# An early-fusion network with two mixture-of-experts layers: plain float32 products on halves of the array's rows instead of high and low parts, and one expert per unit of work

## The reference, cut to what matters

```python
h = concat([patches @ W + b, table[ids] + positions])            # 16 x 548 x 64
h = h + attn0(layernorm(h))     # q, k, v; relu(q k^T * scale) v; a small feed-forward with a relu; layer norms
h = h + moe0(layernorm(h))      # 8 experts, top 1, capacity 1370 tokens per expert: 64 -> 256 -> 64, relu
h = h + attn1(layernorm(h))     # linear attention with grouped norms of k and v, projection, gelu
# moe1: every one of the 8 experts is computed for every token; the two best are weighed
xe = xn[None] * ln_g[:, None] + ln_b[:, None]
hid = gelu(einsum('end,edh->enh', xe, W1) + b1)                  # 64 -> 256
y = einsum('enh,ehd->end', hid, W2) + b2                         # 256 -> 64
h = h + (weights * take(y, top2)).sum()
```

## Time and profile before

| | |
|---|---|
| median of 3 runs | 995.72 us (994.87 to 998.15) |
| span of the profiled execution | 996.3 us |
| busy PE (matmul) | 834.4 us, 84% |
| busy DVE | 691.3 us, 69% |
| busy ACT | 560.5 us, 56% |
| busy POOL | 421.6 us, 42% |
| mean granted TensorE clock | 0.894 of 2.4 GHz |

### The profile page before, as it was taken

The page is one execution under the profiler, slowest core; times in us unless marked ns, Lnnn a source line. Parts: engine busy times, 40 slices in busy tenths (PEclk is TensorE's granted clock), DMA queues, the critical chain, the costliest instruction groups (busy, mean ns, idle before and its releaser), DMA issues.

```text
span 996.3 us, 17997 instructions
## 1 busy us (share of the span) xinstructions
PE 834.4 (84%) x5574; PEld 594.9 (60%) x5574; DVE 691.3 (69%) x2473; ACT 560.5 (56%) x1259; POOL 421.6 (42%) x441
## 2 busy tenths in 40 slices
PE   5799869999987549934589999999999999999995
PEld 3666646666664436614466676666766667666663
DVE  3758789898866525547767778787777777877542
ACT  1366635555543224412266767777777776777773
POOL 4554477674542620046635553455644453110110
PEclk9599879999986569965579999999999999999998
DMA  9700000000000023310000000000000000000000
GB/s 287 218 12 11 10 14 30 23 24 10 5 4 2 6 89 125 109 40 16 6 2 9 2 7 8 7 8 2 7 9 7 9 2 7 8 7 7 1 12 6
DMA packets 36328, 29.06 MB, mean 29 GB/s; under 512 B 18546, under 2 KB 31770, under 8 KB 35850
## 3 DMA queue, kind: packets, MB, share of 16 engines
q1 hardware_dynamic: 27226, 20.59, 6.8%
q0 software_dynamic: 7200, 5.16, 2.1%
q10 hardware_dynamic: 1808, 2.17, 0.6%
HBM read 16.23 MB, written 15.38 MB: 32 GB/s over the span
## 4 chain that ended last, share of the span: by engine, by line
PE 54%; DVE 8%; ACT 7%; issue 4%; DMA 0%; POOL 0%; ACTq 0%; POOLq 0%; DVEq 0%
PE psum L422 12%; PE psum L862 11%; PE psum L863 7%; PE psum L867 4%; PE psum L868 4%; PE psum L435 3%; PE psum L852 3%; PE psum L1039 2%; ACT L511 2%; ACT L464 1%; ACT scratch L511 1%; PE psum L1021 1%; PE psum L360 1%; DVE stats L1213 1%; PE psum L936 1%
## 5 line engine op out<-in xcount | busy, mean ns | idle before, releaser
L511 ACT ACTIVATE scratch<-psum,fb 128x292 f32<-128x292 f32 (+1 forms) x512 | 227.2, 490 | 51.3 <-PE psum L863 50.1
L862 PE MATMUL psum<-xs,fw_hi 128*128 128x292 f32 (+1 forms) x512 | 180.4, 362 | 27.7 <-ACT scratch L511 27.7
L862 PEld LDWEIGHTS psum<-xs,fw_hi 128*128 128x128 f32 x512 | 98.3, 192 | 88.2 <-ACT scratch L511 56.0
L422 PE MATMUL psum<-scratch,w_fw 128*64 128x292 f32 (+1 forms) x1024 | 148.6, 412 | 0.0
L863 PE MATMUL psum<-xs,fw_lo 128*128 128x292 f32 (+1 forms) x512 | 144.9, 293 | 0.0
L302 POOL DMA_INDIRECT uu<-expert_out,slot_i x80 | 84.1, 1051 | 68.7 <-DVE stats L1213 42.5
L852 PE MATMUL psum<-w_ident,hl 128*128 128x128 f32 (+1 forms) x400 | 72.9, 300 | 36.6 <-DVE hl L1222 26.3
L863 PEld LDWEIGHTS psum<-xs,fw_lo 128*128 128x128 f32 x512 | 99.6, 194 | 0.0
L815 POOL DMA_INDIRECT slots_buf<-hl,slot_i x80 | 79.7, 997 | 43.5 <-issue 26.3
L519 ACT ACTIVATE yt<-psum,w_fb 128x256 f32<-128x256 f32 (+1 forms) x128 | 62.6, 489 | 61.8 <-PE psum L422 61.8
L422 PEld LDWEIGHTS psum<-scratch,w_fw 128*64 128x64 f32 x1024 | 62.9, 138 | 42.6 <-issue 12.8
(11 more groups left out here) (289 smaller groups left out, 1996.6 us busy)
## 6 DMA issues: line engine op xcount, KB each, us to landing
slots_buf<-zeros SPq DMA_DIRECT2D x8, 704.0 KB, 8.0
scratch<-slots_buf SPq DMA_DIRECT2D x8, 704.0 KB, 4.4
expert_out<-scratch SPq DMA_DIRECT2D x8, 352.0 KB, 2.5
out<-H SPq DMA_DIRECT2D x16, 128.0 KB
X<-in_patches ACTq DMA_DIRECT2D x1, 1728.0 KB, 7.8
slots_buf<-hl,slot_i POOLq DMA_INDIRECT x80
uu<-expert_out,slot_i POOLq DMA_INDIRECT x80, 2.3
scratch<-in_fw SPq DMA_DIRECT2D x1, 1024.0 KB
```

What stands on the lines that cost most here:

```text
L422: last = pe.matmul(bank(6)[h * D:(h + 1) * D, 0:z - a], w["fw2"][:, (2 * p + h) * J + j, :], hid[(4 * n + 2 * j + h) % 8][:, 0:z - a], sta ...
L511: act.activation(hid[m % 8][:, 0:z - a], bank(up_bank(m))[:, 0:z - a], ACT.Gelu, bias=fb1[:, e * J + j:e * J + j + 1]).then_inc(sem("gelu" ...
L862: pe.matmul(dst, parts[0][:, cols], rhs, start=True, stop=False)
```

## The change

- No high and low parts any more. `turn` transposes pairs of slots: the stack `[128, 292]` has the channels of the even slots' tokens (0, 2, 4: 292 columns) on partitions 0 to 63 and those of the odd slots' (1, 3: 256 columns) on 64 to 127. A batch takes 3 transposes instead of 5. Weights are held twice, on both halves.
- Products over 64 channels are plain float32 matmuls of 64 rows, one per half (`by_sides`, `tokens_by`, `scores`, `q`), which write to different banks (`q`: to different halves of a bank).
- Removed: the casts and subtractions (`high1` to `high3`, `low1` to `low3`, `q_low`, `k_low`, `high_low`, the second half of `fold`), `split_weights`, the splitting of `ew1` and `fw1` in steps 9 and 10, the stage cut1 (16 + 8 steps). `slots_buf` has rows of 64 values instead of 128.
- Banks: TURN (0), FFN (1), WIDE (2, 3), SCORE (4, 5), MIX (6), QUERY (7, also the count), values in (0, 1). The gate uses WIDE. ACT's relu of a `scores(s)` is one operation over both banks.
- Second part: a unit is one batch and one expert, two hidden tiles of 292 + 256 tokens; gelu is one operation over two banks (2 x 292 columns). TensorE's order in a position is up, up, small stage "a", `down` of n-1, `back` of n-2, small stage "b". The orders of the small stages are changed on each engine; DVE does some ahead of `weigh` (`DVE_FIRST`), and mixed and route_b move to positions 6 and 7. `back` ends with a transpose of 64 rows.
- Middle part: `b_turn` has 2 transposes instead of 4; `b_down` and `b_back` have one bank instead of two.

```diff
-        def turn(pe, src, dst_bank, cols=(2 * D)):
-            for s in range(SLOTS):
-                rows = P if s < TXT else N_IMG
-                last = pe.transpose(bank(dst_bank, 2)[0:cols, s * P:s * P + rows], src[0:rows, s, :], ident[0:rows, 0:rows])
+        def turn(pe, src, k):
+            for i in range(3):
+                rows, cols = (P, 2 * D) if i < 2 else (N_IMG, D)
+                last = pe.transpose(bank(k)[0:cols, i * P:i * P + rows], src[0:rows, 2 * i:2 * i + cols // D, :].rearrange("p s c -> p (s c)"), ident[0:rows, 0:rows])
             return last
 
         def turn_back(pe, src, k):
             pe.transpose(bank(k)[:, 0:P], src[:, 0:P], ident[:])
             pe.transpose(bank(k)[:, P:2 * P], src[:, P:2 * P], ident[:])
-            return pe.transpose(bank(k)[0:N_IMG, 2 * P:2 * P + D], src[D:P, LEFT:RIGHT], ident[D:P, D:P])
-
-        def two(pe, dst, parts, rhs, cols=slice(None)):
-
-            pe.matmul(dst, parts[0][:, cols], rhs, start=True, stop=False)
-            return pe.matmul(dst, parts[1][:, cols], rhs, start=False, stop=True)
-
-        def tokens_by(pe, dst, stack, parts, cols):
+            return pe.transpose(bank(k)[0:N_IMG, 2 * P:2 * P + D], src[0:D, LEFT:RIGHT], ident[0:D, 0:D])
+
+        def by_sides(pe, k, weight, stack):
+            for h, z in enumerate(SIDES):
+                half = slice(h * D, (h + 1) * D)
+                last = pe.matmul(bank(k + h)[:, 0:z], weight[half, :], stack[half, 0:z], start=True, stop=True)
+            return last
+
+        def tokens_by(pe, k, stack, weight):
+            n = weight.shape[1]
             for s in range(SLOTS):
-                pe.matmul(dst[:, s, :], stack[:, s * P:(s + 1) * P], parts[0][:, cols], start=True, stop=False)
-                last = pe.matmul(dst[:, s, :], stack[:, s * P:(s + 1) * P], parts[1][:, cols], start=False, stop=True)
+                half, at0, rows = slot(s)
+                i = s // 2 * n
+                last = pe.matmul(bank(k + s % 2)[0:rows, i:i + n], stack[half, at0:at0 + rows], weight[half, :], start=True, stop=True)
             return last
...
+                for h, z in enumerate(SIDES):
+                    half = slice(h * D, (h + 1) * D)
+                    last = pe.matmul(bank(SCORE[h])[0:rows, 0:z], kst[b % 2][half, s % 2, at0:at0 + rows], qst[b % 2][half, 0:z], start=True, stop=True)
+                last.then_inc(sem("scores"), 1)
...
+            def up(n, j):
+                b, e = unit(n)
+                if n % POS == 0 and j == 0:
                     pe.wait_ge(sem("xs5"), b + 1)
...
+                banks.take(pe, (2 + 2 * j, 3 + 2 * j), sem("gelu"), J * n + j + 1)
+                k = (e * J + j) * P
+                by_sides(pe, 2 + 2 * j, w["fw1"][:, k:k + P], xs2[b % 2]).then_inc(sem("up"), 1)
...
                     if now:
-                        up(n, 0, 1)
...
+                        up(n, 0)
+                        up(n, 1)
+                    narrow("a")
+                    if before:
+                        down(n - 1, 0)
+                        down(n - 1, 1)
                     if 0 <= n - 2 < NB * POS:
                         back(n - 2)
-                    if now:
-                        up(n, 3)
-                    if before:
-                        down(n - 1, 0, 1)
+                    narrow("b")
...
-        PE_ORDER = (("norm5", 1, "t5"), ("fold", 2, "gram"), ("norm5", 2, "route"), ("kv", 3, "t4"), ("fold", 3, "gains_k"),
-                    ("fold", 4, "gains_v"), ("fold", 5, "by_q"), ("kv", 5, "kv"), ("fold", 6, "by_proj"), ("fold", 7, "proj"))
...
+        PE_ORDER = (("fold", 1, "b", "gram"), ("norm5", 2, "a", "t5"), ("fold", 2, "b", "gains_k"), ("kv", 3, "a", "t4"), ("fold", 3, "b", "gains_v"),
+                    ("norm5", 4, "a", "route"), ("fold", 4, "b", "by_q"), ("kv", 5, "a", "kv"), ("fold", 5, "b", "by_proj"), ("fold", 6, "b", "proj"))
...
+            def gelu(n, j):
+                b, e = unit(n)
+                act.wait_ge(sem("up"), J * n + j + 1)
+                if n >= 2:
+                    act.wait_ge(sem("down"), n - 1)
+                act.activation(hid[(J * n + j) % 4][:], both(2 + 2 * j), ACT.Gelu, bias=fb1[:, e * J + j:e * J + j + 1]).then_inc(sem("gelu"), 1)
...
+        DVE_FIRST = (("fold", 2, "gram_s"), ("fold", 3, "p1_s"), ("fold", 4, "own_heads"), ("fold", 5, "add_input"), ("fold", 6, "fold"), ("fold", 7, "pre_bias"))
+        DVE_ORDER = (("fold", 1, "kvnorm"), ("norm5", 1, "norm5"), ("kv", 2, "norm4"), ("norm5", 4, "route_a"), ("kv", 5, "kv_b"),
+                     ("kv", 6, "sum_squares"), ("mixed", 6, "mixed"), ("fold", 7, "resid2"), ("norm5", 7, "route_b"))
```

More of the change, by code:

```diff
@@ L6 @@
 F32 = mybir.dt.float32
-F32R = mybir.dt.float32r
 BF16 = mybir.dt.bfloat16
@@ L402, in up @@
-            def up(n, *tiles):
-                b, side, p = unit(n)
-                a, z, _, _ = PARTS[side]
-                if n % POS == 0 and 0 in tiles:
-                    pe.wait_ge(sem("xs5"), b + 1)
-                for k in tiles:
-                    j, e = k // 2, 2 * p + k % 2
-                    m = up_bank(4 * n + k)
-                    banks.take(pe, (m,), sem("gelu"), 4 * n + k + 1)
-                    two(pe, bank(m)[:, 0:z - a], split["fw1"], xs2[b % 2][:, a:z], slice((e * J + j) * P, (e * J + j + 1) * P)).then_inc(sem("up"), 1)
@@ L414, in down @@
-            def down(n, *tiles):
-                b, side, p = unit(n)
-                a, z, _, _ = PARTS[side]
-                if 0 in tiles:
-                    banks.take(pe, DOWN, sem("ysb"), n + 1)
-                for j in tiles:
-                    pe.wait_ge(sem("gelu"), 4 * n + 2 * j + 2)
-                    for h in range(2):
-                        last = pe.matmul(bank(6)[h * D:(h + 1) * D, 0:z - a], w["fw2"][:, (2 * p + h) * J + j, :], hid[(4 * n + 2 * j + h) % 8][:, 0:z - a],
-                                         start=(j == 0), stop=(j == J - 1))
-                if J - 1 in tiles:
+                tokens_by(pe, 0, xs2[b % 2], w["wr"]).then_inc(sem("route_prod"), 1)
@@ L425, in down @@
                     last.then_inc(sem("down"), 1)
             def back(n):
-                b, side, p = unit(n)
-                _, _, s0, s1 = PARTS[side]
                 banks.take(pe, BACK, sem("weigh"), 2 * n + 1)
                 pe.wait_ge(sem("ysb"), n + 1)
-                for s in range(s0, s1):
-                    rows = P if s < TXT else N_IMG
-                    k = (s - s0) * P
-                    last = pe.transpose(bank(7)[0:rows, k:k + P], ysb[n % 2][:, k:k + rows], ident[:])
@@ L436, in back @@
-                last.then_inc(sem("back"), 1)
+                turn_back(pe, ysb[n % 2], 7).then_inc(sem("back"), 1)
             for step in range(STEPS2):
-                K, F, W5 = (at2(step, k) for k in ("kv", "fold", "norm5"))
                 for pos in range(POS):
@@ L900, in q_or_k @@
                 pe.wait_ge(sem("xs1"), b + 1)
-                for h in range(2):
-                    last = two(pe, bank(2 + h)[:, 0:HALF], split[name], xs1[b % 2][:, h * HALF:(h + 1) * HALF])
+                for h, z in enumerate(SIDES):
+                    half = slice(h * D, (h + 1) * D)
+                    last = pe.matmul(bank(7)[half, 0:z], w["wq"][half, 0:D], xs1[b % 2][half, 0:z], start=True, stop=True)
                 last.then_inc(sem("qk_prod"), 1)
-            def q(b):
-                q_or_k(b, "wq")
```

589 lines of the change are left out of this document (235 added, 354 removed).

## The result

The changed kernel takes 1077.2 us (median of 4 runs, 1067.0 to 1090.1), the kernel before beside it 996.9: a ratio of 1.076 (1.071 to 1.082). Forecast were 965 us. The profiled execution has a span of 1073.7 us against 996.3, 77.4 us more.

A forecast was written before the change was run, and what follows sets the result against it. TensorE's order of work was taken to bound both long stretches. First part -32 us, between and the second part's first steps -8, second part +9 took 996.3 to 965 us (950 to 982, at 0.5).

The forecast's parts named there:

- part 4: Waits: in the first part LOW's goes; in the second `back` waits about 1.5 us, counted +0.4 us per batch.
- LOW's 1.06 us: First part: TensorE's wait per step for bank LOW, held by the count's reader, goes since ffn2 has its own bank.
- one step less: First part, before the pipeline is full: stage cut1 goes, between 0 and -16 us, taken as -6.
- the step of 27.5 us: First part: POOL's weight operations delay the next gather; that step takes 27.6 us instead of 16.65, so -11 us.
- The halved transfers: Ahead of the first `b_turn`: `slots_buf` at half size halves its transfers, between 0 and -6 us, taken as -3.
- the two DVE operations taken away: Second part's first steps: chains lose two operations of 0.49 us twice per step; with fewer transposes, -5 us.
- part 2: Changes of form: a second-part unit takes 2.69 us against 2.6, +0.6 us per batch of 8; first part -0.2 per step.
- Part 1: Products over 64 channels: row halves overlap, 0.49 us per tile as now; overlapping weight loads save 0.45 us per group.
- the two ends: Products over 64 channels: a tile costs 0.49 us if row halves overlap, 0.93 us if they don't.
- (a): Products over 64 channels: row halves don't overlap, each tile costs 0.43 us more, 1165 us; chance 0.12.
- (b): Slower through changes of form and the second part's positions 6 to 0: +45 us instead of +9, 1012 us; chance 0.14.
- (c): Second part gets faster, loads overlapping and late gelus caught up: -1 us per batch, 940 us; chance 0.2.

The follow-up runs named there:

- e2: Changed kernel with both new waits removed: values and gate write banks 6 and 7, ffn2 bank 6, attend bank 1; 968.5 us, ratio 0.974.
- e6: Kernel of e2 with the second product of each pair also on rows 0 to 63, so row halves cannot overlap; 1408.7 us, ratio 1.416.
- e12: Changed kernel, both waits kept, with six dummy bfloat16 matmuls ahead of each of the two; 991.5 us, ratio 0.993.
- e3: Kernel before with both waits put in: values product to bank 1, gate to bank 2; 1080.2 us, one run.
- e11: Kernel before with v's wait alone added, for ACT's copy behind t2; 1034.3 us, ratio 1.034.
- e7: Kernel of e2 with t2 moved behind count in TensorE's order; 1008.0 us, ratio 1.016.
- e9: Kernel of e2 with dummy bfloat16 matmuls in the second part's first four steps; 977.4 us (957.0 to 995.0).
- e8: Kernel of e2 with four dummy bfloat16 matmuls ahead of t2 in each step of the first part; 965.6 us, ratio 0.970.
- e10: Kernel of e2 with the dummy matmuls of both e8 and e9; 969.9 us, ratio 0.973.

## Why the prediction was wrong, step by step

**The step that failed** is in part 4. Part 4 named for the first part only the wait that goes (LOW's 1.06 us) and said "what is late next is TensorE itself". The diff had the two new ones in the open: VALUE is banks (0, 1) and TURN is (0,), t2 stands directly ahead of v in the order, and the gate writes WIDE directly ahead of k. Each stage that moved had to be asked who reads its new bank last; I did so for ffn2, which gained, and not for v and k. The second failure is that the clock of 1.00 went through all sums of the two long stretches as a constant. The prediction named a clock below 1.00 as what would make it wrong and gave it no case, no price and no chance; a stretch busy 108 of 116 us with one wait of 1.06 us per step looked safe. Priced, it would have been the rival on the slow side: 15 steps at half clock are 15 x (26 - 15) = 165 us at worst; it came to +70 against the old kernel.

**What the prediction says of the change without these two waits is e2**: 968.5 us measured, 965 forecast. Its profiled span is 34.8 us below that of before, where the sum had -31:
- First part up to the last count: -46.1 (forecast -32). The first count comes 7.6 us earlier (one step less: forecast -6), the step of 27.5 us is gone (forecast -11), the full steps are 14.3 to 15.2 instead of the forecast 15.4: DVE, which I expected to give some of the gain back, is at its bound only here. Against this stand about 13 us that the stretch at 0.50 costs (steps of 20.0 and 21.8).
- Between, middle and first steps of the second part: +1.1, +2.1 and +0.6, where -3, 0 and -5 were forecast. The halved transfers and the two DVE operations taken away brought nothing that these stages show; why is not shown.
- Units and tail of the second part: +7.5 (forecast +9), but not for the forecast reason (part 2).

That 968.5 stands so near to 965 is in part luck: the first part gained 14 us more than forecast, and the stages between it and the units cost 3.8 us where a gain of 8 was forecast.

**Part 1** was right. The row halves overlap: 1.17 us for two hidden tiles against 2.04 in e6, so 0.43 us per tile, the distance of the two ends that I had named. The loads of the two halves overlap as well: the ten passes of `proj` last from 730.24 to 731.06, 0.82 us. The last transpose of `back` starts with them, at 730.23, and takes 0.16 us in the earlier trace rows; without it they last 0.66, where 0.67 was forecast for this case and 1.12 for the other. The Trainium skill, TensorE: Matmul & The Clock Gate (Packing small matmuls), says that products on distinct row groups run concurrently; the prediction could show no row for it, and here the trace agrees.

**Part 2** had the unit right, 2.69 to 2.75 us for 2.69. Its own pieces for today's unit add up to 2.59, so the difference per batch of 8 is +0.8, not the +0.6 that it states; this changes nothing in the total, which took +0.6 per batch for work that the pieces had left out. That term came out near the measured one by luck. A batch of the changed kernel takes 31.4 us over its last ten batches against 31.1 before, but at full clock it takes 30.5 against 30.8: faster by 0.3, near what the pieces had said (-0.25 as stated, -0.05 with the +0.8). The rest is the clock again. Three batches of the changed kernel have 10 us at 0.50 in them (from 609.0, 704.6 and 800.1 us) and take 34.6 or 34.7; before, the stretches at 0.50 there are 3.4 us long. Each of the three falls comes 1.1 to 1.3 us behind the end of `back`'s wait of 1.62 us, the one of part 4; that wait stands in the other batches too.

**Part 4, second part**, had the mechanism and not quite its split. `back` was to wait about 1.5 us per batch for weigh, mostly within the gelu's wait. From 630 to 1000 us, twelve batches, the waits of TensorE are:

```profile
PE psum L774 <- DVE tmp L670: 22.0, 23, 2.3
PE psum L781 <- ACT hid L455: 8.8, 11, 1.3
```

That is 1.8 us per batch for weigh and 0.7 for the gelu, 2.5 together, the sum that was forecast; but the wait for weigh is the longer one, and most of it is in the open.

**The rivals.** (a) falls: e6 shows that it would have been even dearer than 1165 us. (b) named the right sign for the wrong reason: its place was the second part, which took 3.4 us more, and its 1012 us were not reached by way of it. (c) falls: the second part did not get faster, though at full clock a batch did, by 0.3 of the 1 us that it named.

## What to carry to other kernels

When a change moves outputs between PSUM banks, list for each writer of each bank who reads it last and what stands directly ahead of that writer in TensorE's order; a wait of about a microsecond per step there can cost far more than itself. Give the clock a term of its own in the sum, with a price (the difference of the stretch at either level) and a chance, as soon as a change adds a recurring wait of TensorE to a stretch that DVE or the latency nearly fills. To see whether a loss is of this kind, look at the granted clock by stretch before anything else, and try dummy work in the place of the wait: if the time falls, it was the clock.

## What the runs showed of the hardware that I had not expected

With two waits of 0.9 to 1.2 us per step of 24 to 26 us, and TensorE busy in 92% of the time (139.8 of 151.6 us), the granted clock had a mean of 0.53. Without them (e2 up to 165 us) or with work in their place (e12) it was 1.00. A wait of that length once per step is not enough by itself: the kernel before has one of 0.81 to 1.06 us in each step of a stretch at 1.00, and e2 has t3's of 0.72 to 1.24 us up to 165 us, at 1.00. The Trainium skill, TensorE: Matmul & The Clock Gate (A second HAM failure mode: psum-queue depth-cycling), tells of a kernel in which short idles between groups of matmuls, from cycling through PSUM banks, made the clock go back and forth. The kernel before with these waits (e3, mean 0.70, and e11, 0.82) does that; the changed kernel does more, it stays down but for short rises.

The clock can stay at 0.5 for 126 us (e7) and over 100 (e9) while TensorE is busy for 100 and 99% of the time by its records. The kernel before was busy for 93% of a stretch at 1.00. So a busy share read from the records doesn't tell what clock will be granted. With the old products it came back within 7 us mostly (e11), with full-array dummy matmuls once per step within 10 (e8, two falls). What of the new products does it is not settled: they use 64 rows each, they are plain float32 instead of float32r, and they came in together, with another order of the stages; no run parts these. e6 adds that products on one row half only, one after the other, keep it low throughout the first part, though in the second part, beside `down`'s full-height products, it ran at 1.00 (125.6 of 130 us busy from 820 to 950 us).

The first part of e2 runs near that edge: with the same first part e9 gave 957 to 995 us, where the spread of the kernel before was 992.6 to 999.8. Of all kernels run, e8 (965.6), e2 (968.5) and e10 (969.9) beat both the kernel before and the changed one; they can't be told apart.
